# Moving the lower half of the low part's products behind the next slot's minus points

## The reference

```python
def _L0_conv_ref(x, w_route, b_route, w_experts, ...):
    pooled = jnp.mean(x, axis=(2, 3))
    routing = jax.nn.sigmoid(pooled @ w_route.T + b_route)
    y = conv(x, w_experts)                     # 4 experts, 3x3, 128 -> 128
    out = jnp.einsum('beohw,be->bohw', y, routing)
    ...                                        # batch norm
    return jax.nn.silu(out)
...
x = x + _L0_conv_ref(_gn(x), ...)
x = x + conv(_gn(x), jnp.sign(W))              # 3x3, 128 -> 128
```

## Time and profile before

| | before |
|---|---|
| median of three runs | 278.58 us (278.16 to 278.6) |
| the profiled execution, its own time | 279.2 us |
| its span, first to last instruction | 277.4 us |
| granted TensorE clock | 0.999 of full speed |
| TensorE busy | 271.6 us, 98% |
| VectorE busy | 245.6 us, 89% |
| ScalarE busy | 207.4 us, 75% |
| GpSimd busy | 52.0 us, 19% |

### The profile page before, as it was taken

The page is one execution under the profiler, slowest core; times in us unless marked ns, Lnnn a source line. Parts: engine busy times, 40 slices in busy tenths (PEclk is TensorE's granted clock), DMA queues, the critical chain, the costliest instruction groups (busy, mean ns, idle before and its releaser), DMA issues.

```text
span 277.4 us, 4010 instructions
## 1 busy us (share of the span) xinstructions
PE 271.6 (98%) x1322; PEld 187.8 (68%) x1322; DVE 245.6 (89%) x443; ACT 207.4 (75%) x417; POOL 52.0 (19%) x59
## 2 busy tenths in 40 slices
PE   8999989999999999999999999999999999999996
PEld 7854846859586776859576675858576675848554
DVE  5879999999999999999999999999999999992732
ACT  2487988886969788787979788796989795537750
POOL 2000011214122041414123041414112021312000
PEclk9999999999999999999999999999999999999999
DMA  6999825443535545361735544361544545270422
GB/s 230 393 395 300 282 116 151 66 103 70 113 108 76 151 79 131 56 119 76 114 114 78 151 74 105 70 132 77 95 135 76 152 77 116 50 140 2 76 76 78
DMA packets 11397, 34.68 MB, mean 125 GB/s; under 512 B 1264, under 2 KB 3568, under 8 KB 11376
## 3 DMA queue, kind: packets, MB, share of 16 engines
q0 software_dynamic: 4032, 14.68, 31.1%
q1 hardware_dynamic: 7056, 19.47, 18.9%
q10 hardware_dynamic: 288, 0.26, 0.3%
HBM read 11.34 MB, written 15.73 MB: 98 GB/s over the span
## 4 chain that ended last, share of the span: by engine, by line
PE 88%; DVE 6%; ACT 3%; issue 1%; POOL 0%; ACTq 0%; DVEq 0%; POOLq 0%
PE pc L496 40%; PE pa L461 13%; PE pb L461 13%; PE pe_ L461 12%; PE pd L451 4%; PE pd L405 3%; DVE U L969 1%; PE ps L431 1%; PE pb L496 1%; PE ps L435 1%; ACT y L761 1%; DVE U L959 1%; PE ps L423 1%; DVE sums L1044 0%; DVE X L1076 0%
## 5 line engine op out<-in xcount | busy, mean ns | idle before, releaser
L496 PE MATMUL pc<-lo,ws 128*128 128x496 f16 (+5 forms) x288 | 64.7, 371 | 0.0
L969 DVE SCALAR_TENSOR_TENSOR U<-we,route,U 128x1152 f32<-128x1152 f32 x45 | 63.7, 1416 | 0.1
L496 PE MATMUL pc<-hi,ws 128*128 128x496 f16 (+5 forms) x288 | 62.8, 372 | 0.2 <-ACT hi L770 0.2
L366 POOL TENSOR_TENSOR rstd<-ve,nhalf 128x2 f32<-128x2 f32 (+1 forms) x19 | 26.0, 1368 | 138.3 <-ACT ve L686 136.7
L496 PEld LDWEIGHTS pc<-hi,ws 128*128 128x128 f16 x288 | 28.1, 98 | 31.0 <-issue 0.6
L496 PEld LDWEIGHTS pc<-lo,ws 128*128 128x128 f16 x288 | 28.4, 105 | 25.5
L461 PE MATMUL pa<-V,UM 128*128 128x256 f32 (+1 forms) x180 | 41.7, 382 | 0.0
L461 PE MATMUL pe_<-V,U 128*128 128x256 f32 (+1 forms) x180 | 40.6, 375 | 0.0
L461 PE MATMUL pb<-V,UM 128*128 128x256 f32 (+1 forms) x180 | 40.5, 375 | 0.0
L461 PEld LDWEIGHTS pb<-V,UM 128*128 128x128 f32 x180 | 34.2, 190 | 5.4 <-issue 0.5
L461 PEld LDWEIGHTS pe_<-V,U 128*128 128x128 f32 x180 | 34.1, 190 | 3.8
(11 more groups left out here) (116 smaller groups left out, 392.0 us busy)
## 6 DMA issues: line engine op xcount, KB each, us to landing
X<-x SPq DMA_DIRECT2D x15, 512.0 KB, 5.2
out<-X SPq DMA_DIRECT2D x14, 512.0 KB, 2.6
X<-y POOLq DMA_DIRECT2D x14, 512.0 KB, 4.5
out<-ev POOLq DMA_DIRECT2D x14, 512.0 KB, 5.3
we<-w_experts SPq DMA_DIRECT2D x3, 768.0 KB, 7.8
out<-X SPq DMA_DIRECT2D x3, 256.0 KB, 2.0
ws_raw<-w_sign SPq DMA_DIRECT2D x1, 576.0 KB, 11.2
X<-x ACTq DMA_DIRECT2D x2, 128.0 KB, 3.0
```

The costliest lines, as they stand in the source:

```text
L366: g.tensor_tensor(rstd[:, c, a:b], ve[:, c, a:b], nhalf[:, a:b], ALU.pow).then_inc(rstd_ready, 1)
L496: mm = mm_(rows[:, r0 - first // W:r1 - first // W, c0:c1], ws[:, tap * C:(tap + 1) * C], (hi, lo)[part][i % 2][:, r0 + ky - 1:r1 + ky - 1 ...
L969: v.scalar_tensor_tensor(out=flat(U[i % RING][:]), in0=flat(we[:, e, :, :]), scalar=route[:, i, e:e + 1], in1=flat(U[i % RING][:]), op0=AL ...
```

## The change

On TensorE the last nine products of an image, the low part of the lower half, leave the end of their slot. They stand in the next slot behind the minus points, five before the variance product and four behind it. The mean product, which stood between the low products of the two halves, now stands among those of the upper half. In slot 1 there are no such products to take over, and slot 15 still computes all of image 14.

On ScalarE `mean_in` is moved ahead of `silu`, and `var_in` ahead of `routing` and `mix`. On VectorE `mix(t + 1, 2)` is moved ahead of the inverse transform (not in slot 1), and `pool_routes` ahead of `low_part`.

```diff
@@ tensor @@
                 if t < B:
+
                     minus_points(t)
                     if t == 1:
                         group_means(c)
                     else:
+                        sign_half(t - 2, 1, 1, TAP_ORDER[:5])
                         group_vars(c)
+                        sign_half(t - 2, 1, 1, TAP_ORDER[5:])
                     plus_points(t)
@@
                     sign_half(t - 1, 0, 1)
                     if c < B:
                         route_logits(c)
-                    sign_half(t - 1, 1, 0)
+                    sign_half(t - 1, 1, 0, TAP_ORDER[:5])
                     group_means(c + 1)
-                    sign_half(t - 1, 1, 1)
+                    sign_half(t - 1, 1, 0, TAP_ORDER[5:])
@@ scalar @@
                 if c < B:
                     normalise(c)
+                if c + 1 < B:
+                    mean_in(c + 1)
                 silu(t)
                 if t < B - 1:
                     mean_mid(t)
                 if c + 1 < B:
-                    mean_in(c + 1)
+                    var_in(c + 1)
                 if c < B:
                     routing(c)
                     mix(c)
-                if c + 1 < B:
-                    var_in(c + 1)
@@ vector @@
                 mix(t + 1, 1)
+                if t > 1:
+                    mix(t + 1, 2)
                 inverse_sums(t)
                 inverse_inner(t)
                 inverse_outer(t)
+                pool_routes(t + LAG - 1)
                 low_part(t - 1)
-                mix(t + 1, 2)
-                pool_routes(t + LAG - 1)
+                if t == 1:
+                    mix(t + 1, 2)
                 mix(t + 1, 3)
```

## The result

The changed kernel takes 282.23 us by the median of six runs (281.77 to 283.28) against 278.4 for the kernel before, measured again beside it. The ratio is 1.0129, with a 95% interval of 1.0109 to 1.0149: slower, by 3.6 us of 278.4 (the two medians differ by 3.8). The span of the profiled execution is 280.1 us against 277.4.

The account below looks back on a forecast made before the run. TensorE, 98% busy, bounds the kernel, the chain round the engines having 0.3 us to spare. Start +0.35, eleven intervals +1.3, slots 14 and 15 +0.03 - 0.08, end +0.74: +2.4 us, median 281.0, range 278.2 to 285.0.

Parts of the forecast that it names:

- TensorE's own slot: TensorE's time per slot without waits: 15.65 us against 15.73, with 0.08 us of weight load gained.
- The chain through mean_in: Loop from one variance product to the next, mean_in's 1.04 us ahead of SiLU: 15.85 us a slot; chance 0.52, 280 to 283.
- a late residual: Bound: a residual landing 0.2 us later a round adds half of it, +1.1 us, 282.1.
- The 0.1 us that decides: Whether GpSimd's power is asked for before VectorE's mix 1 starts (16.2 to 16.3) or after (16.3 to 16.4).
- Rival A: TensorE sets the slot: power asked for before mix 1 takes 0.7, chain 15.5; 278.6, no change; chance 0.20.
- The start: Slot 1 to slot 2: SiLU of slot 1 later, variance product of slot 2 at 49.15 against 48.80, +0.35 us.
- the 1.34: Wait of 1.34 us of slot 1's logits for pooled behind mix 2: goes, but is turned into other waits.
- a cover of 0.7 us: Spare time before the mean product needs the previous routing, 10.4 against 11.2 us behind the variance product.
- Rival B: Faster: covered weight load and the logits' lost wait, slot 2 some 1 us earlier; 277.6 (-0.35%); chance 0.12.
- Rival C: Chain longer than computed, chance 0.16: 283 to 285, or one in four power passed over at mix 1's end, 297.
- Cover of the moved parts: Low part, pooled route and logits keep over 1 us each; copy to ev is done before nbias at about 2.5.
- a filled gap: On VectorE, mix 2 (1.33 us) fills the gap before the sums left by later plus points; VectorE does not grow.

Follow-up runs that it names:

- e1: The changed kernel with ScalarE's order of before (mean_in behind SiLU, var_in behind mix), TensorE and VectorE still changed: ratio 1.001 to the kernel before.
- e11: The changed kernel with two added unused VectorE instructions of 4 columns ahead of mix 1 from slot 2 on: ratio 1.0056 to the kernel before.
- e4: The kernel before with only ScalarE's new order (mean_in ahead of SiLU, var_in ahead of routing and mix): ratio 1.0028.
- e3: The changed kernel with VectorE's mix 1 directly behind all_rows, ahead of inner rows and transforms, from slot 2 on: ratio 1.0125 to the kernel before.
- e9: e3 with a wait on a long satisfied semaphore in front of each of VectorE's three last transforms: ratio 1.0143 to the kernel before.
- e7: The kernel before with pool_routes ahead of the low part and mix 2 in slot 1 alone: ratio 0.998.
- e5: The changed kernel with VectorE's order of before (mix 2 and pooled behind the low part): 289.17 us, ratio 1.0367 to the kernel before.
- e6: The changed kernel with extra unused fp32 products on TensorE in slot 1, ahead of the mean product: ratio 1.0072 to the kernel before.

## Why the prediction was right, and where it was off

**Direction and range.** Slower was forecast at 0.68, with 281.0 and 278.2 to 285.0; 282.23 came. The forecast was +2.4 us, the measured ratio is +3.6 and the two traces +3.7. Of the 1.3 between forecast and traces, 1.0 is the start and 0.4 the intervals; the rest of the sum held within 0.1.

**TensorE's own slot** came as computed: 15.64 in natural intervals (15.65), the variance product at 3.62, the plus points at 381 ns, and 0.74 more behind the last variance product (0.74).

**The chain through mean_in** is the cause of the longer intervals: e1 and e11 take it away from two sides. The power alternated, 1.88 where the variance product had not waited and 1.14 to 1.56 where it had, and intervals such as 15.75 and 15.92 in slots 7 to 11 average 15.83, against 15.85 predicted. The whole row gives 15.88. I sized it at +1.3 and it was +1.73: in slots 3 and 11 the square of the residual began 6.5 us after SiLU and not 6.2, and in slot 6 the power was slow although the variance product had waited. The sum had no term for either; a late residual stood only among the bounds. The waits of TensorE at the variance product were put at 0.1 to 0.3 us; they reached 0.47 in slot 4, and slots 14 and 15 lost nothing.

**The 0.1 us that decides.** Rival A named it, and e11 shows both sides of it. The prediction read the earlier trace rows against the earlier trace rows as 0.02 against 0.04 us ahead of the mix; e4 and slots 12 and 13 of the kernel before have 0.71 at 0.02 as well, so this distance doesn't decide. That a power asked for inside a mix ends 0.57 or 0.58 behind its end held in every slot of the changed kernel. For VectorE's instructions at large, which is how e3 put it, the rule is wrong (e3, e9). The forecast got by with it because in the changed kernel the instruction in progress is the mix, which is in part luck.

**The start** is the step that was mis-sized: +0.35 was forecast and +1.36 came. The forecast of SiLU 1.04 later and the variance product 0.35 later holds within 0.11: without the low clock slots 1 to 2 take 15.73 (e9), 0.46 more than before. The other 0.90 is the granted clock after TensorE's idle time, for which the sum had no term. I had seen that waits take the place of the 1.34, gave the mean product's wait for the routing a cover of 0.7 us in the steady slots, and did not work it out for slot 1, where it is 1.84. The wait that was to come before the minus points of slot 2 did not: the row of 44.82 has none.

**Rival B** asked for a quick power and an earlier slot 2. e7 has the second without the rest of the change and is worth 0.2%. **Rival C's** passing over at mix 1 did not occur in 14 slots of the changed kernel.

**Cover of the moved parts** held: low part, hi, the copy to ev and the mean product of the steady slots never made TensorE wait. e5 shows the price of the one cover that I called a filled gap, 0.48 us a slot on top of the changed kernel.

## What to carry to other kernels

A row of an engine that is 98% busy can still be one step from another bound: add up the loop that goes once round all engines, compare it with the slot, and count what is to spare before putting anything into it. Here 0.3 us was to spare and 1.04 was put in. Look in such a loop for a step whose time hangs on two requests that nearly coincide. Work out every new wait for the first slots separately, where the cover of the steady state isn't there.

## What the runs showed of the hardware

- GpSimd's power takes 0.55 us for one column (slots before the first, kernel before); for two columns it took 0.71 at the least and up to 2.04 beside VectorE (e9). At the same distance from the mix, to a hundredth of a microsecond, it is 0.71 or 2.01 (e4 against the earlier trace rows). The Trainium skill (SBUF — State Buffer, "Who interferes with whom") says that the second to issue is blocked until the first has finished. The trace agrees where the power is asked for inside a mix: 1.87, ending 0.57 behind it (the changed kernel). It doesn't show an order of first come, first served: in the earlier trace rows the power was asked for 0.02 ahead of the mix and was still held to its end, and in e3 it was held past the ends of up to three short instructions.
- After an idle time of 1.84 us TensorE's granted clock fell to 0.50 (the changed kernel; 0.69, 0.50 and 0.96 in three stretches of 2 us, from 42 us on) in three profiled executions and stayed at 1.00 in a fourth of the same slot (e9). With eight added instructions ahead of the wait and 0.95 us of wait left it stayed at 1.00 (e6).
- The fp32 products of 256 columns behind the product of two columns took 400 ns in the mean, 0.08 us a slot more than with fp16 products in between (381). That the fp32 weight load is what costs this is argued from the page of the profile (a load takes 190 ns in fp32 and 98 in fp16, the small pair issues for 0.14 us) and not shown by a run of its own.
